# A gated delta-rule layer on one core: the small blocks' X and the last scaling move to ScalarE, and the last turn of outputs moves behind the second level of the inverse

## The reference, cut to what matters

```
xn  = layernorm(x)                                    # 4 batches, 512 tokens, width 256
q, k, v, z = split(xn @ W_qkvz.T);  b, a = split(xn @ W_ba.T)
q, k, v = silu(causal 4-tap convolution of (q, k, v)) # 16 heads of q and k, 32 of v, width 128
beta, g = sigmoid(b), -exp(A_log) * softplus(a + dt_bias)
per head, in 8 chunks of 64 tokens (rows 0..63 of a chunk):
    decay = exp(cumsum g differences), lower triangle
    M = strictly lower part of (k beta) k^T * decay
    T = inverse of (I + M)                            # 64 x 64, unit lower triangular
    v_c, k_cumdecay = T (v beta),  T (k beta exp(g))
    v_new = v_c - k_cumdecay state
    out   = (q exp(g)) state + (q k^T * decay) v_new
    state = state * exp(g_last) + (k exp(g_last - g))^T v_new
s   = (norm_w * rmsnorm(out) * silu(z)) @ W_out.T
ffn = down(silu(gate(xn)) * up(xn)), weights = a table of 16 values read by index
result = x + s * silu(ffn)                            # float32 throughout
```

## Time and profile before

| | |
|---|---|
| time, median of 3 runs | 2369.5 us (2366.62 to 2370.72) |
| the profiled execution's own time | 2362.46 us |
| its span, first to last instruction | 2360.7 us |
| mean granted TensorE clock | 0.976 |
| busy: PE, DVE, ACT, POOL | 93%, 72%, 52%, 73% |

### The profile page before, as it was taken

One profiled execution on the slowest core, in us unless ns is written; L12 is line 12 of the kernel. 1 busy time (PEld: TensorE's weight loads), 2 busy tenths in 40 slices (PEclk: granted clock), 3 DMA queues, 4 the chain that ended last, 5 costly groups with the idle time before them and its releaser, 6 DMA issues.

```text
span 2360.7 us, 76348 instructions
## 1 busy us (share of the span) xinstructions
PE 2200.7 (93%) x32208; PEld 1693.1 (72%) x32208; DVE 1703.7 (72%) x3403; ACT 1238.6 (52%) x2949; POOL 1733.0 (73%) x1774
## 2 busy tenths in 40 slices
PE   3799999999999999999999999999999999999898
PEld 2677777777777777777777777777777777776554
DVE  6777777777877777777877777778777677786322
ACT  3665555565555555655555546655555556554111
POOL 2787877788887787878887777888887778788100
PEclk8899999999999999999999999999999999999999
DMA  3111111111111110111111101111121101111100
GB/s 97 47 41 34 45 36 28 26 45 36 44 32 34 45 36 19 36 45 32 40 41 34 45 10 44 36 45 32 33 45 36 30 25 45 36 36 42 37 18 18
DMA packets 70949, 87.44 MB, mean 37 GB/s; under 512 B 16720, under 2 KB 39376, under 8 KB 70608
## 3 DMA queue, kind: packets, MB, share of 16 engines
q1 hardware_dynamic: 70608, 82.55, 13.5%
HBM read 77.45 MB, written 5.08 MB: 35 GB/s over the span
## 4 chain that ended last, share of the span: by engine, by line
PE 60%; DVE 24%; ACT 7%; issue 5%; POOL 2%; DMA 1%; SPq 0%; DVEq 0%; POOLq 0%; ACTq 0%
PE ps_p L671 8%; PE ps_two L454 7%; PE ps_two L429 5%; PE ps_state L429 4%; PE ps_p L611 4%; DVE cacc L989 3%; DVE terms L1091 3%; PE ps_state L635 3%; PE ps_p L584 3%; PE ps_p L619 3%; PE ps_p L503 3%; PE ps_state L503 2%; ACT qg L786 2%; PE ps_p L454 2%; PE ps_p L720 2%
## 5 line engine op out<-in xcount | busy, mean ns | idle before, releaser
L1335 POOL TENSOR_TENSOR Sd<-St,el 128x512 f32<-128x512 f32 x192 | 201.3, 1048 | 328.0 <-DVEq L1236 328.0
L1374 POOL TENSOR_SCALAR Kg<-idx_s,lutb 128x134 f32<-128x134 int32 x480 | 371.6, 777 | 27.1
L1215 DVE TENSOR_SCALAR Vn<-ps_p,bR 128x128 f32<-128x128 f32 x512 | 167.8, 350 | 211.4 <-PE ps_p L584 136.9
L671 PE MATMUL ps_p<-w_o,hT 128*128 128x256 f32 x992 | 258.5, 407 | 51.7 <-DVEq L1258 51.7
L989 DVE SCALAR_TENSOR_TENSOR cacc<-ps_state,cw,cacc 128x1022 f32<-128x1022 f32 (+2 forms) x192 | 244.4, 1273 | 15.5 <-DVE XW L1168 7.4
L989 DVE SCALAR_TENSOR_TENSOR cacc<-ps_two,cw,cacc 128x1022 f32<-128x1022 f32 (+2 forms) x192 | 245.2, 1277 | 11.0 <-ACT cacc L753 2.6
L671 PEld LDWEIGHTS ps_p<-w_o,hT 128*128 128x128 f32 x992 | 191.6, 200 | 82.1 <-DVE hT L1255 54.2
L429 PE MATMUL ps_state<-xnT,w_qkv 128*128 128x256 f32 x1024 | 237.4, 385 | 6.0 <-DVEq L994 5.9
L429 PE MATMUL ps_two<-xnT,w_qkv 128*128 128x256 f32 x1024 | 241.5, 390 | 0.7 <-DVEq L994 0.7
L429 PEld LDWEIGHTS ps_state<-xnT,w_qkv 128*128 128x128 f32 x1024 | 193.7, 192 | 34.0 <-DVEq L994 6.5
L429 PEld LDWEIGHTS ps_two<-xnT,w_qkv 128*128 128x128 f32 x1024 | 194.3, 195 | 27.3 <-DVEq L994 0.8
(11 more groups left out here) (191 smaller groups left out, 5374.9 us busy)
## 6 DMA issues: line engine op xcount, KB each, us to landing
qg<-g_scratch SPq DMA_DIRECT2D x64, 512.0 KB, 7.4
g_st<-g_scratch SPq DMA_DIRECT2D x64, 256.0 KB, 5.8
w_qkv<-in_wqkvz SPq DMA_DIRECT2D x16, 512.0 KB, 3.8
w_z<-in_wqkvz SPq DMA_DIRECT2D x16, 256.0 KB, 3.2
w_o<-in_wout SPq DMA_DIRECT2D x16, 256.0 KB, 2.9
idx_s<-in_idx SPq DMA_DIRECT2D x32, 67.0 KB, 1.8
fw_scratch<-looked_up SPq DMA_DIRECT2D x32, 67.0 KB, 2.0
Kg<-in_x SPq DMA_DIRECT2D x2, 1024.0 KB, 5.7
```

The source lines that it names most:

```text
L671: m = pe.matmul(bank[:, b * D:(b + 1) * D], hT[:, t, b, 1 - a, :], w_o[:, a, :], start=(a == 0), stop=(a == RATIO - 1))
L1215: dve.tensor_scalar(Vn[:, cur, b], bank[:, 0:P], bR[:, R.par, b, c:c + 1], None, ALU.mult).then_inc(done, 1)
L1335: pool.tensor_tensor(Sd[:, :, :, :], St[:, c % 2, :, :, :], el[:, R.par, :, :, c].unsqueeze(3).broadcast_to([P, BB, RATIO, P]), ALU.mult). ...
L1374: m = pool.tensor_scalar(slots[k], idx_s[:, :], float(k), lutb[:, k:k + 1], ALU.is_equal, ALU.mult)
```

## The change

X's two halves are written by ScalarE (`small_x`), ahead of the swap, as soon as `base` has reached 23; VectorE goes from W straight to the taps. The counter `xs` then counts four writes a round instead of five, and `x_in` the two of ScalarE. The last turn's scaling moves from VectorE's `begin` to ScalarE (`scale_last`, four activations), behind its copies of the next round's first two transposed v. TensorE turns it back behind the second level's products instead of before the first turn of outputs, and VectorE gates it there. The taps of each kind stand in one piece. The projections 6 and 7 move from the middle of the second level to its end, the third turn of outputs the other way. The first transposed v goes to bank 1 instead of bank 3, and the last turn-back is now bank 4's use behind the second turn of outputs. GpSimd starts the second batch's `scale_q` only when the first step of the next round's `small_blocks` is done.

```diff
-PROJ_AT = {(4, 1): (4, 5), (5, 0): (6, 7)}
-OUT_AT = {(4, 0): (1,), (4, 1): (2,), (5, 1): (3,)}
+PROJ_AT = {(4, 1): (4, 5), (5, 1): (6, 7)}
+OUT_AT = {(4, 0): (1,), (5, 0): (2,), (5, 1): (3,)}
@@ bank_uses
-             + spread([("vt", i) for i in range(4)], (3, 7, 4, 5)))
+             + spread([("vt", i) for i in range(4)], (1, 7, 4, 5)))
-    outs = [] if first else [(("ot3", 0), 4)] + spread([("out", i) for i in range(4)], (5, 4, 5, 4))
+    outs = [] if first else spread([("out", 0), ("out", 1), ("out", 2), ("ot3", 0), ("out", 3)], (5, 4, 5, 4, 4))
@@ TensorE, invert
                 if R.before() is not None:
-                    turn_back(R.before(), 3)
                     outputs(R, "out", R.before(), 0)
                 for n, lv in enumerate(LEVELS):
-                    pe.wait_ge(s["xs"], R.at(1 + 3 * n, 0, 5))
+                    pe.wait_ge(s["xs"], R.at(1 + 2 * n, 0, 4))
@@ TensorE, beside
+                if R.before() is not None and (lv, half) == (5, 1):
+                    turn_back(R.before(), 3)
@@ TensorE, keys_through
-                    pe.wait_ge(s["xs"], R.at(5, 0, 5))
+                    pe.wait_ge(s["xs"], R.at(4, 0, 4))
@@ TensorE, turn_back
-                pe.wait_ge(s["scaled"], R.at(i + 1, 0, 4))
+                if i < 3:
+                    pe.wait_ge(s["scaled"], R.at(i + 1, 0, 3))
+                else:
+                    pe.wait_ge(s["scaled_3"], R.at(1, 0, 1))
@@ ScalarE, invert
                 if R.nxt:
                     tap0(R, 1)
+                small_x(R)
                 swap(R, 0)
@@ ScalarE
+            def small_x(R):
+
+                act.wait_ge(s["base"], R.at(23, 0, 23))
+                x = X.rearrange("p b c (q i) -> p (b c) q i", q=2)
+                for q in range(2):
+                    act.activation(x[:, :, q, :], blocks[:, :, :], ACT.Copy, scale=in_half[q]).then_inc(s["x_in"], 1)
+
+            def scale_last(R):
+
+                act.wait_ge(s["inv_o"], R.at(4, 0, 4))
+                bank, done = wait_full(act, R, "o", 3)
+                for u in range(4):
+                    m = act.activation(on[:, 3, u * P:(u + 1) * P], bank[:, u * P:(u + 1) * P], ACT.Copy,
+                                       scale=rr[:, 3, u // BB, u % BB:u % BB + 1])
+                m.then_inc(s["scaled_3"], 1)
+                act.wait_ge(s["scaled_3"], R.at(1, 0, 1))
+                act.sem_inc(done, 1)
+
             def swap(R, n):
 
-                act.wait_ge(s["xs"], R.at(2 + n, 0, 5))
+                if n == 0:
+                    act.wait_ge(s["x_in"], R.at(2, 0, 2))
+                else:
+                    act.wait_ge(s["xs"], R.at(2, 0, 4))
@@ ScalarE, body
                 if R.nxt:
                     begin(R.following())
+                scale_last(R)
@@ VectorE, begin
-                if last is not None:
-                    scale_o(last, 3)
@@ VectorE, small_blocks
-                m.then_inc(xs, 1)
-                for q in range(2):
-                    m = dve.tensor_scalar(x[:, :, q, :], blocks[:, :, :], in_half[q], None, ALU.mult)
                 m.then_inc(xs, 1)
@@ VectorE, invert
                 if R.nxt:
-                    taps(R, 0, (1,))
-                if of is not None:
-                    gated(of, 3)
-                if R.nxt:
-                    taps(R, 0, (2, 3))
+                    taps(R, 0, (1, 2, 3))
                 if of is not None:
                     outputs(R, "out", of, 0)
-                second_products(R, 4, 3)
+                second_products(R, 4, 2)
                 turn()
                 if R.nxt:
                     taps(R, 1, (1, 2, 3))
                 else:
                     hidden(0, 0, AHEAD[0])
+                    hidden(1, 1, AHEAD[1])
                 if of is not None:
                     outputs(R, "out", of, 1)
+                second_products(R, 5, 4)
+                if of is not None:
+                    gated(of, 3)
+                    outputs(R, "out", of, 2)
                 if R.nxt:
                     taps(R, 2, (1, 2, 3))
-                if of is not None:
-                    outputs(R, "out", of, 2)
-                if not R.nxt:
-                    hidden(1, 1, AHEAD[1])
-                second_products(R, 5, 5)
-                if R.nxt:
                     taps(R, 3, (1, 2, 3))
@@ VectorE, body, last round
                     gated(R, 2)
-                    scale_o(R, 3)
                     gated(R, 3)
@@ GpSimd, body
                 if R.nxt:
                     scale_q(R, 0)
+                    pool.wait_ge(s["base"], R.following().at(1, 0, 23))
                     scale_q(R, 1)
```

More of the change, by code:

```diff
@@ L222, in build @@
         names = ("ld_x ld_const ld_idx ld_w ld_wz ld_wo ld_round ln_stat ln_std ln_inv ln_xn ln_t ln_T ln_xp ln_Ta ba_mm "
-                 "ba_act g_c g_dup g_tr g_sc g_out fw_c fw_st ld_fw ld_fd zeroed tap0 taps silu sq n2_c rinv_c inv_o turned scaled "
+                 "ba_act g_c g_dup g_tr g_sc g_out fw_c fw_st ld_fw ld_fd zeroed tap0 taps silu sq n2_c rinv_c inv_o turned scaled scaled_3 x_in "
                  "normed_o dec_pool dec_small ss_c dec_act qg_c sd_c kg_c a_c u_c base blk_t xs st_c x_c o_sq ff_gu ff_gate ff_h ff_y ff_sy fin x_again stored").split()
@@ L1137, in small_blocks @@
                 dve.wait_ge(s["blk_t"], R.at(1, 0, 1))
-                w, x = (t.rearrange("p b c (q i) -> p (b c) q i", q=2) for t in (W, X))
+                w = W.rearrange("p b c (q i) -> p (b c) q i", q=2)
                 for q in range(2):
                     m = dve.tensor_scalar(w[:, :, q, 0:BASE], wb[:, :, 0:BASE], in_half[q], None, ALU.mult)
-                m.then_inc(xs, 1)
-                for q in range(2):
-                    m = dve.tensor_scalar(x[:, :, q, :], blocks[:, :, :], in_half[q], None, ALU.mult)
                 m.then_inc(xs, 1)
@@ L1205, in second_products @@
                 into_odd(lv, ps_p1[:, :, S // 2:S].rearrange("p b (q n) -> p b q n", n=1 << lv)).then_inc(xs, 1)
-                dve.wait_ge(xs, R.at(n, 0, 5))
+                dve.wait_ge(xs, R.at(n, 0, 4))
                 for b in range(BB):
@@ L1246, in scale_o @@
                                   ).then_inc(s["scaled"], 1)
-                dve.wait_ge(s["scaled"], R.at(i + 1, 0, 4))
+                dve.wait_ge(s["scaled"], R.at(i + 1, 0, 3))
                 dve.sem_inc(done, 1)
```

## The result

The changed kernel takes 2306.84 us (median of 4, 2302.22 to 2309.52) against 2370.11 us before (median of 4): 0.9725 times, 95% interval 0.9693 to 0.9757. The forecast was 2284, its range 2264 to 2325. So the sign is right and the time lies in the range, but 63 us were gained where 86 were forecast, and the forecast's own range, without the rivals, ended at 2300. The profiled execution took 2307.89 us (span 2306.1, mean granted clock 0.986).

A forecast was written before the change was run, and what follows sets the result against it. TensorE's idle before the inverse's first products and second outputs (2.52 us a round) and the clock drops bound it; 52.5 us idle plus 30 us clock off 2362.46 gives 2280, plus half the 7.0 us median offset 2284, range 2264 to 2325.

The forecast's parts named there:

- The chain to W: VectorE's serial steps from L1062 to W: scaling gone and GpSimd held back, W 1.04 us earlier.
- The term of L1068: Later step of VectorE's chain to W, with two SBUF inputs: 0.2 us charged for meeting GpSimd's third multiplication.
- the lock: Rival, chance 0.12: both held-back GpSimd multiplications go ahead of L1068, W comes 0.2 us later than now; 2323 us.
- ScalarE: ScalarE takes X (1.2 us) and four scalings (1.21 us) into its idle time; P1 stays covered by 0.7 us.
- The sum of a clean round: Keys' products 2.05 us earlier, taken as 1.75 us a round (bounds 1.0 and 2.1), 52.5 us over 30 rounds.
- by these times it doesn't wait: VectorE, with two output adds and six taps queued behind the moved turn-back's gating, was forecast to have no wait.
- under 0.4 us: Sign: new short waits, among them the keys' products (L576) for VectorE's last add (L1264), each below this size.
- The clock: Granted clock drops behind TensorE's idle stretches, costing some 35 us in all, go mostly with the long idle.
- 30 of the 35 us: The part of the clock drops' cost forecast to go with the long idle stretch ahead of the outputs.
- The clock keeps dropping: Rival, chance 0.12: small products and remaining waits still bring the clock to 0.50; only 52.5 us gained, 2313 us.
- Slower: Rival, chance 0.05: the moved turn-back holds VectorE, keys wait for its last add; at 3 us of wait, 2400 us.

The follow-up runs named there:

- with bank 3: The changed kernel with the last turn of outputs in bank 3 in place of bank 4: 2249.65 us, 0.9463 times the kernel before.
- the blocks' ends out of the way: The changed kernel with 30 empty waits more a round and an offset of 294 ahead of the first round: 2292.96 us, 0.9645 times the kernel before.

## Why the prediction was right, and where it was short

**The chain to W** was right in its mechanism: L1087 starts where it was forecast and takes what it was forecast to take. The term of L1068 was too dear: 0.2 us charged, none paid; the other 0.2 us by which W leads the forecast lie in W itself. The run without GpSimd's wait shows both what the wait buys (0.75 us a round) and that the lock would have gone to L1068. The Trainium skill (SBUF — State Buffer, Who interferes with whom) fits: L1093 has two SBUF inputs and takes 1.0 us longer beside a scaling.

**ScalarE** was right: X takes 1.32 us on it and 0.90 on VectorE (0.82 until the next instruction starts), and yet the round is 0.29 us shorter with X on ScalarE, 0.63 with bank 3, since ScalarE has idle time there and VectorE hardly any. The Trainium skill (ScalarE: Activation LUTs, Rules for kernel authors) sends multiplications to VectorE; by duration the rows agree, by the round's length they do not.

**The sum of a clean round** was mis-sized: "I take 1.75 us a round" measured 1.49, 30 x 0.26 = 8 us. The step was "by these times it doesn't wait": VectorE does wait, 0.50 us in nearly every round, for the second level's products, because the move puts that copy ahead of two groups of taps. So its last add is 0.36 us later than forecast although W comes 0.41 us earlier; TensorE is 0.4 us earlier, and the keys wait for the difference. They wait also for the 0.25 us from the add's end to their start, which its rows show (1114.60 to 1114.85) and the prediction left out. Its sign "under 0.4 us" for this wait came out at 0.97.

**The clock** was the larger miss: "30 of the 35 us" came back as 7 or 8 net. The step failed, not its reason: the drops behind the long idle did go. What I did not see is the block of instructions. The row was there (the waits of L576 on "issue" in the kernel before), and I did not ask what it was. The keys' products wait for VectorE's last add, in the kernel before too, where the wait ends as late but costs TensorE only 0.05 us; until then the sequencer gets no further, the next block is asked for only then, and the keys' 256 instructions run in 2.1 us where, in the stall at 632.36, it took 4.5 us from the keys' start (630.47) until TensorE went on, and 3.7 in the next round, without the weights. With the blocks' ends out of the way, and less the offset's own 10.6 us, the kernel takes 2282, two less than forecast. The Trainium skill (Runtime: NRT & Kernel Launch, Instruction fetch mechanics) calls the cost of crossing a block mostly hidden; the runs show it hidden, 0 us, where the sequencer can run ahead, and up to 3.2 us a block where a wait stops it just before dense small products.

That the sequencer is held at that wait and asks behind it is inferred from when the wait ends and the packet starts; how far ahead TensorE asks was not measured by itself. Why the stalls doubled is open: in rounds 8, 16, 24 and 25 of the kernel before the packet starts 4.8 to 6.3 us ahead of the keys, behind an earlier wait, and in the changed kernel, at the same places, behind the keys' start.

**The rivals.** "The lock" needs the kernel without GpSimd's wait. "The clock keeps dropping" came true in size, by another cause; the time lies in the stated range only because its upper end took in such rivals, and that is luck. "Slower" named the right place, VectorE behind the moved turn-back, at 0.5 us instead of 3. That the move could be worth less than nothing was not among them: without it the kernel is 1.4% faster, since ScalarE's part had already taken the idle from 1.69 to 0.32 us. It pays only together with bank 3: the two make the best kernel of all (0.9463).

## What to carry to other kernels

When two edits aim at one stall, work out each alone: here the engine relief removed most of the stall, and the reordering brought a new chain; it paid only once the last turn of outputs had another bank. Before moving work to the end of a stage, look at which bank the next stage opens first and who reads it last. And ask of every "issue" wait in front of dense small matmuls whether it is the instruction queue: count the instructions of a round against the block.

## What the runs showed of the hardware

TensorE's instructions come in packets of 256 (256 packets for 65,519). Some 130 instructions that do nothing, ahead of the first round, moved the time from 2378.5 to 2293 us, 3.6%, although they take 8 us themselves: by where the blocks end, and by nothing else. A stall of 1.5 us in the keys' products cost 1.8 us where the clock held; where it fell to 0.50, 1.6 to 3.3 us came on top. Idle of 2.1 us in one piece brought that fall in 9 of 30 rounds; the 0.83 and 1.69 us of the kernel before, 1.1 us apart, in 15 of 30; of 0.97 us, in rounds without a stall, in none.
